# One PSUM tile for all of the attention, an FFN output that lands by token, four search steps in every body, and two FFN pieces at a body's front

## What is computed

```python
x = x + _xattn(_layernorm(x), ctx, ctx, mask, WQ, bQ, WK, bK, WV, bV, Wp, bp)
x = x + _ffn(_layernorm(x), W1, b1, W2, b2, gamma, beta, Wr, br)
# _xattn: softmax((Q K^T) * mask) / sqrt(d) @ V, then @ Wp + bp
# _ffn:   probs = softmax(layernorm(x) @ Wr + br)
#         out = sum_e probs[e] * (gelu(x @ W1s[e] + b1s[e]) @ W2s[e] + b2s[e])
# W1s[1:], b1s[1:], ...: the largest 5% by |w| times 0.2, the smallest 5% times 1.8
```

## Time and profile before

| | us |
|---|---|
| median of 3 runs | 839.43 |
| lowest and highest | 836.33, 840.46 |
| the profiled execution | 837.27 |
| its span, first to last instruction | 835.5 |
| PE busy / weight loads busy | 718.3 / 605.3 |
| DVE busy / ACT busy / POOL busy | 525.4 / 316.0 / 291.2 |

### The profile page before, as it was taken

One profiled execution on the slowest core, in us unless ns is written; L12 is line 12 of the kernel. 1 busy time (PEld: TensorE's weight loads), 2 busy tenths in 40 slices (PEclk: granted clock), 3 DMA queues, 4 the chain that ended last, 5 costly groups with the idle time before them and its releaser, 6 DMA issues.

```text
span 835.5 us, 15333 instructions
## 1 busy us (share of the span) xinstructions
PE 718.3 (86%) x5346; PEld 605.3 (72%) x5346; DVE 525.4 (63%) x1327; ACT 316.0 (38%) x428; POOL 291.2 (35%) x288
## 2 busy tenths in 40 slices
PE   3438758898898859989989989989896999999996
PEld 2426656787787748878878878888674888888884
DVE  3698468547857976776776776666499334333441
ACT  1302201333442324444444444443352444555442
POOL 2246034225625732762753753735381000000000
PEclk9758757679799959999999999979897999999999
DMA  5851510420341115044044033023020122222121
GB/s 162 192 136 51 112 43 22 96 66 27 101 109 32 51 54 115 27 111 105 26 119 98 25 104 90 26 76 102 26 77 15 61 76 75 75 75 72 41 63 50
DMA packets 128571, 62.36 MB, mean 75 GB/s; under 512 B 101520, under 2 KB 118800, under 8 KB 128528
## 3 DMA queue, kind: packets, MB, share of 16 engines
q1 hardware_dynamic: 128528, 61.81, 28.0%
HBM read 34.51 MB, written 23.09 MB: 69 GB/s over the span
## 4 chain that ended last, share of the span: by engine, by line
PE 66%; DVE 21%; issue 6%; POOL 4%; ACT 1%; DMA 0%; DVEq 0%; ACTq 0%; POOLq 0%
PE ps_y L337 8%; PE ps_y L338 8%; PE ps_y L339 8%; PE ps_l L337 7%; PE ps_l L338 7%; PE ps_l L339 7%; PE ps_m L591 6%; DVE ind L1212 5%; POOL xh L993 3%; PE ps_m L678 3%; PE ps_s L337 2%; PE ps_s L339 2%; PE ps_s L338 2%; DVE region_a L1113 2%; PE ps_m L626 2%
## 5 line engine op out<-in xcount | busy, mean ns | idle before, releaser
L874 ACT ACTIVATE region_b<-ps_l,bias 128x512 f32<-128x512 f32 x128 | 88.1, 689 | 196.7 <-PE ps_l L339 193.7
L1025 POOL TENSOR_TENSOR region_c_lo<-region_b,region_c_hi 128x512 fp32r<-128x512 f32 x64 | 98.0, 1547 | 142.9 <-ACT region_c_hi L877 142.9
L1212 DVE TENSOR_SCALAR ind<-key,cand 128x2048 bf16<-128x2048 uint16 x124 | 116.1, 978 | 5.0 <-PE ps_m L678 3.0
L1442 DVE TENSOR_TENSOR region_c_lo<-region_b,region_c_hi 128x512 fp32r<-128x512 f32 x64 | 44.1, 692 | 109.0 <-ACT region_c_hi L877 104.6
L337 PE MATMUL ps_l<-x2s_hi,w_hi 128*128 128x512 f32 x256 | 108.0, 422 | 5.0 <-DVE x2s_lo L1076 5.0
L678 PE MATMUL ps_m<-ones_bf,ind 128*128 128x1 bf16 x1984 | 63.2, 164 | 51.6 <-DVE ind L1212 48.2
L337 PE MATMUL ps_y<-region_c_hi,w_hi 128*128 128x512 f32 x256 | 103.9, 406 | 1.6 <-POOL region_c_lo L1025 1.6
L678 PEld LDWEIGHTS ps_m<-ones_bf,ind 128*128 128x128 bf16 x1984 | 58.4, 99 | 62.7 <-DVE ind L1212 56.4
L338 PE MATMUL ps_l<-x2s_lo,w_hi 128*128 128x512 f32 x256 | 103.5, 404 | 0.0
L339 PE MATMUL ps_l<-x2s_hi,w_lo 128*128 128x512 f32 x256 | 103.4, 404 | 0.0
L339 PE MATMUL ps_y<-region_c_hi,w_lo 128*128 128x512 f32 x256 | 101.6, 397 | 0.0
(11 more groups left out here) (173 smaller groups left out, 1232.8 us busy)
## 6 DMA issues: line engine op xcount, KB each, us to landing
acc_scr<-acc SPq DMA_DIRECT2D x8, 514.0 KB, 4.8
acc<-acc_scr SPq DMA_DIRECT2D x8, 514.0 KB, 3.3
xa<-in_x SPq DMA_DIRECT2D x8, 512.0 KB, 5.2
q_scr<-qn_hi SPq DMA_DIRECT2D x16, 256.0 KB, 4.5
q_scr<-qn_lo SPq DMA_DIRECT2D x16, 256.0 KB, 4.6
qs_hi<-q_scr SPq DMA_DIRECT2D x8, 512.0 KB, 4.1
qs_lo<-q_scr SPq DMA_DIRECT2D x8, 512.0 KB, 5.0
x<-in_x SPq DMA_DIRECT2D x32, 128.0 KB, 3.6
```

The costliest lines, as they stand in the source:

```text
L874: act.activation(g[:, f % 4, :], ps_l[:, f % 2, :], ACT.Gelu_apprx_tanh, bias=bias[:, e, f:f + 1]).then_inc(s["gelu"].handle, 1)
L1025: pool.tensor_tensor(gs[1][:, f % 4, :], g[:, f % 4, :], gs[0][:, f % 4, :].bitcast(F32), ALU.subtract).then_inc(s["g_lo"].handle, 1)
L1212: dve.tensor_scalar(ind[s % 2][:], key[:, key_of[rnd][s], :], cand[:, s:s + 1], None, ALU.is_le).then_inc(ind_ready.handle, 1)
L1442: dve.tensor_tensor(gs[1][:, f % 4, :], g[:, f % 4, :], gs[0][:, f % 4, :].bitcast(F32), ALU.subtract).then_inc(s["g_lo"].handle, 1)
```

## The change

1. **PSUM.** The turned probabilities, the turned queries' input and the queries move from `ps_l` and `ps_y` into `ps_s`, which also holds scores, turned output, projection and turned x2. `ps_l` and `ps_y` belong to the FFN alone. New waits keep the users of `ps_s` apart.
2. **FFN output by token.** `output` takes the GELU tile as the stationary operand and W2 as the moving one: 12 matmuls of 256 columns in place of 6 of 512. `bias_y` and `turn_y` go. b2 is added by a new `base` on VectorE (4 operations a batch).
3. **Scores.** `sc` gets four tiles and the exponential is taken in place. All four scores of batch i+1 are made at the end of body i, all four of batch 0 in the prologue.
4. **Search.** There are four steps in each of bodies 0 to 6 and none in body 7. Four `ind` tiles; the small arrays take one comparison and one reduction; `decide` forms the next candidate in its second operation.
5. **Order.** Two FFN pieces, h(0) and h(1), stand at the front of a body, and the GELUs stand between the attention's copies on ScalarE. `mix` stands before `mask_scores(i+1, 3)`.
6. **Prologue.** The keys of batch 0 go straight into `kbd` (`load_first_keys`, 16 small DMAs). The loads are reordered, and the steps stand between the masks.
7. `normalise_output` takes one four-dimensional operation a tile.
8. The weights' perturbation takes up `probabilities`, `base` and the b2 row between its parts.

```diff
-            for m in range(DC):
-                mm = three(pe, ps_y[:, m, :], [w[:, f * D + m * P:f * D + (m + 1) * P] for w in w2s],
-                           [t[:, f % 4, :] for t in gs], f == 0, f == FC - 1)
+            for t in range(NT):
+
+                mm = three(pe, ps_y[:, t // 2, (t % 2) * D:(t % 2) * D + D], [a[:, f % 4, t * P:(t + 1) * P] for a in gs],
+                           [w[:, f * D:(f + 1) * D] for w in w2s], f == 0 and t % 2 == 0, f == FC - 1 and t % 2 == 1)
...
         def turn_queries_input(b):
 
             wait(pe, ln[0]["xhat"], b)
-            wait(pe, ex[0]["mixed"], b - 3)
+            if not isinstance(b, int) or b > 0:
+                wait(pe, pT_ready, b - 1, 1)
...
             wait(pe, xT_lo, b)
+            if not isinstance(b, int) or b > 0:
+                wait(pe, pT_ready, b - 1, 2)
...
-        def turn_probs(b, j):
+        def turn_probs(b, j, last=False):
+
             wait(pe, p_exp, b, j + 1)
             if j == 0:
-                wait(pe, ex[0]["g_hi"], b - 2)
-            elif j < NT - 1:
+                wait(pe, s_masked, b)
+            elif j == 1 and not last:
+                wait(pe, xT_lo, b + 1)
+            elif j == 2 and not last:
+                wait(pe, q_lo, b + 1)
+            else:
                 wait(pe, pT_ready, b, j)
...
+            h(0)
+            h(1)
+            turn_probs(i, 0, last)
+            if not last:
+                turn_queries_input(i + 1)
+            values(i, 0)
+            c(0)
+            turn_probs(i, 1, last)
+            if not last:
+                queries(i + 1)
+            values(i, 1)
+            t(0)
+            h(2)
...
+            probs(i, NT - 1)
+            if not first:
+                router_exp(i - 1)
+            more_gelu(0)
             turned(i, 0)
...
+            if not last:
+                decide(k + 2)
+                mask_scores(i + 1, 0)
+                mask_scores(i + 1, 1)
+                compare(k + 3, rnd)
+            low_x2(i)
+            if not last:
+                mask_scores(i + 1, 2)
+            logits(i)
+            if not last:
+                counts(k + 3)
+            if not first:
+                mix(0, i - 1)
+            if not last:
+                mask_scores(i + 1, 3)
+                decide(k + 3)
```

More of the change, by code:

```diff
@@ L694, in keys_values @@
                 mm.then_inc(kv_product, 1)
-        def step(k):
-            count(k, 0)
-            count(k, 1)
-            total(k)
         pe.wait_ge(ld_ctx, 16)
@@ L708, in _ @@
         pe.wait_ge(ctx_lo, 1)
-        keys_values(0, ps_s)
+        keys_values(0, ps_l)
         turn_queries_input(0)
-        keys_values(1, ps_l)
         pe.wait_ge(proj_lo[0], 1)
         queries(0)
+        keys_values(1, ps_y)
         pe.wait_ge(kk_in, 16 * B)
+        pe.wait_ge(kv_biased, KC)
         for c in range(DC):
             for k in range(KC):
-                mm = pe.transpose(ps_s[:, c, k * P:(k + 1) * P], kk[:, k, c * P:(c + 1) * P], ident[:])
+                mm = pe.transpose(ps_l[:, c, k * P:(k + 1) * P], kk[:, k, c * P:(c + 1) * P], ident[:])
         mm.then_inc(k_turned, 1)
         pe.wait_ge(consts_ready, 5)
-        for k in range(AHEAD):
-            step(k)
+        count(0)
+        pe.wait_ge(proj_lo[3], 1)
+        pe.wait_ge(k0_lo_in, 16 * HH)
+        wait(pe, q_lo, 0)
+        scores(0, 0)
+        total(0)
+        scores(0, 1)
+        count(1)
+        scores(0, 2)
+        total(1)
+        scores(0, 3)
         pe.wait_ge(route_w, 2 * DC)
@@ L727, in _ @@
         mm.then_inc(route_sum, 1)
-        pe.wait_ge(proj_lo[3], 1)
-        pe.wait_ge(k_lo, 1)
-        scores(0, 0)
-        scores(0, 1)
-        scores(0, 2)
+        count(2)
+        total(2)
         pe.wait_ge(route_ready, 1)
         def body(i, rnd, first=False, last=False):
-            k = step_of(i, rnd)
-            more = not isinstance(i, int) or i + 2 < B
-            turn_probs(i, 0)
-            scores(i, 3)
-            values(i, 0)
-            if not last:
-                turn_queries_input(i + 1)
-            turn_probs(i, 1)
-            count(k, 0)
-            if not last:
-                queries(i + 1)
-            values(i, 1)
-            count(k, 1)
-            turn_probs(i, 2)
-            turn_probs(i, 3)
-            total(k)
-            values(i, 2)
+            k = step_of(i)
             def h(f):
@@ L1059, in body @@
                 normalise(0, i + 2, xa)
+            for f in range(3, FC - 2):
+                low(f)
+            rsqrt(1, i)
+            normalise(1, i, x2)
+            low(6)
+            if not last:
+                shift(i + 1, 0)
+            low(7)
+            if not last:
+                shift(i + 1, 1)
+            router_rsqrt(i)
             if not last:
@@ L1362, in body @@
                     dve.tensor_copy(key[:, 2 + n, :], halfword(wraw[:, n, :], 0)).then_inc(key_ready, 1)
-            compare(k + 1, 0, rnd)
+            else:
+                probabilities(i - 1)
+                base(0, i - 1)
             normalise_output(i, 2)
-            normalise_output(i, 3)
-            if not first:
-                probabilities(i - 1)
-            low_output(i)
-            compare(k + 1, 1, rnd)
-            counts(k + 1)
-            add_residual(i)
-            stats(1, i, x2)
-            decide(k + 1)
-            compare(k + 2, 0, rnd)
-            compare(k + 2, 1, rnd)
-            counts(k + 2)
-            decide(k + 2)
-            if rnd == 0 or last:
-                step(k + 3, rnd)
-            if more:
+            if not isinstance(i, int) or i + 2 < B:
                 wait(dve, x_in, i + 2)
@@ L1383, in body @@
             if not last:
+                counts(k + 1)
+            normalise_output(i, 3)
+            if not last:
+                decide(k + 1)
+                compare(k + 2, rnd)
+            low_output(i)
+            if not last:
+                counts(k + 2)
+            add_residual(i)
+            stats(1, i, x2)
+            if not last:
+                decide(k + 2)
                 mask_scores(i + 1, 0)
-            logits(i)
-            if not last:
                 mask_scores(i + 1, 1)
+                compare(k + 3, rnd)
             low_x2(i)
@@ L1423, in last_expert @@
             split_x2(0)
-            for part, s in ((slice(0, FC), 4), (slice(FC, FC + DC), 6)):
-                perturb(bias[:, 1, part], bias[:, 0, part], sabs[:, part], tier[:, part], s, pb_ready)
             wait(dve, ex[0]["y_step"], B - 1)
             split([t[:] for t in w2s], wagain[:, 1, :], pw_hi, 2, pw_lo)
-            probabilities(B - 1)
-            mix(0, B - 1, ps_s)
+            mix(0, B - 1)
         pipeline(dve, body, second_round, last_expert)
@@ L1436, in perturbed_expert @@
                 split_x2(b)
+                mix(1, b - 1)
             for f in range(FC):
-                if f == 2 and not first:
-                    mix(1, b - 1, ps_m)
                 wait(dve, s["g_hi"], b, f + 1)
```

479 lines of the change are left out of this document (240 added, 239 removed).

## The result

The changed kernel took **909.41 us** (median of 4 runs, 906.8 to 911.69). Beside them the kernel before took 837.88 (4 runs, 836.27 to 840.46). The ratio is 1.085, with a 95% interval from 1.080 to 1.090. The forecast was 904, slower, in a range from 864 to 934.

A forecast was written before the change was run, and what follows sets the result against it. Full bodies and expert 1 were taken as bound by TensorE, the prologue and body 0 by latency and queues. Terms 17.4 + 10.8 + 50.6 - 8.8 + 2.6 - 7.6 = +65 took the 835.5 span to 900.5, median 904; range 864 to 934.

The forecast's parts named there:

- the wait at the front: At a full body's start TensorE waits about 7 us for ScalarE's copy of the turned probabilities, behind a 9.4 us chain.
- Six full bodies: Bodies 1 to 6: 75 us each, from 59.0 work and 15.9 waits, plus 6 once; 456 in all, +50.6 us.
- the second round: Second round of the search, on VectorE behind the fourth mask: 13.1 us before, only 6 remain, in one full body.
- The wait at `total`: At a full body's end TensorE waits 4 us for VectorE's counts, and 1 more ahead of the last count.
- The smaller waits: Within a full body, TensorE's waits at turned probabilities, queries' low part, second step's total and queries' input: together 3.9 us.
- the price of the clock: In a full body, half-rate values, count and queries after the front's wait: up to +5 us, as a bound only.
- Four comparisons near the end: VectorE's four comparisons near a body's end, slowed beside GpSimd's low parts and shifts: 5 to 6 us, not 2.8.
- Prologue: Before the bodies: mask at 69 to 70, then 21 us on VectorE; first turned probabilities at 90, not 72.6: +17.4 us.
- Body 0: First body, without FFN to fill waits: first copy 8 us after the transposes, 75.5 us against 64.7, +10.8.
- Body 7 and the way to expert 1: Body 7: 52 us from 60.8, -8.8; weights' perturbation on VectorE before expert 1: 37 instead of 34.5, +2.6.
- Expert 1: Last stage: output by token costs nothing, dropping `turn_y` gives 0.7 in each of 7 batches, the end 2.6: -7.6 us.
- the work alone sets the body: Rival, chance 0.12: the front's chain is covered, full bodies take 62 us, and the kernel takes 807.

The follow-up runs named there:

- e5_order: e1_front with an FFN piece and the last output piece moved between narrow matmuls on TensorE, and the fourth mask ahead of `mix` on VectorE: 855.7 us.
- e4_prologue: e1_front with batch 0's mask loaded before the queries' store, search steps ahead of the scores, and GpSimd normalising batch 1 before the first subtraction: 844.7 us.
- e8_two: The changed kernel with the values normalised in two three-dimensional operations a tile again: 909.6 us, against 907.4 for the changed kernel beside it.
- e6_both: The edits of e4_prologue and e5_order together on e1_front: 830.7 us, ratio 0.989 to the kernel before.
- e10_input: e9_total with normalisation and the queries' input's low part ahead of a body's first comparisons on VectorE, and the first count behind the queries on TensorE: 816.4 us.
- e1_front: The changed kernel with ScalarE's copies of the first turned probabilities and queries' input ahead of the first GELUs, the former also ahead of the fourth exponential: 867.0 us.
- e9_total: e6_both with the last total behind the next body's first FFN piece on TensorE, and last counts and fourth mask ahead of the router's logits on VectorE: 837.7 us.

## Why the prediction was right

The sign, the size and the main mechanisms were right: 904 forecast and 909 measured, with the wait at the front and the late prologue where they were forecast. But in the largest term two errors of the same size cancelled, and that part is luck.

- **Six full bodies**: 456 forecast, 456.2 measured, of them 74.6 to 74.9 us for three of the five without the second round. *Split wrong.* I had put 59.0 us of work and 15.9 of waits. It was 65.2 of work and 9.7 of waits. The wait at the front was 6.1 (forecast 7), through the chain forecast: 9.35 us from mask to transposes, of 9.4. The wait at `total` was 0.3 to 0.4 in four of the six bodies and 1.7 and 1.9 in the other two, not 4, and the one ahead of the last count was nil, not 1. The smaller waits were 3.2 of 3.9. So the waits had been put 6.2 too high. Against that stands the price of the clock, the step that failed: I named up to +5 as a bound for it and put nothing in the sum, and TensorE was busy for 6.2 us more than forecast, with 17 us at 1.2 GHz at the front and 3 more at the end. By the 57.7 us of the same matmuls at 2.4 GHz (e5_order) the clock even cost 7.5, and the work had been put 1.3 too high. The missing wait at `total` and the slow clock are in part the same thing: in the body from 400.2 the scores ahead of it ran at half rate from 468.0 on and so came nearly as late as VectorE did, while in the body from 243.3, where no half-rate stretch stood there, the wait was 1.7. The second round added 7.5 us to its body, not 6.
- **Four comparisons near the end** took 4.91 us (forecast 5 to 6), but not by being slower each, as I had reckoned. The shortest, the median and the longest of the four, in ns:

```profile
L1220 DVE TENSOR_SCALAR ind<-key,cand x4: 741/742/2926, 460.2 to 464.4; 128x2048 bf16<-128x2048 uint16 x4
```

  One took 2.93, beside a low part and a subtraction of GpSimd, and three took 0.74, as they do alone. The pair of 2.71 in the earlier trace rows is made in the same way, of 2.04 and 0.74. What was mis-sized for the wait at `total` is when VectorE would be through the logits: 21.6 us after the projection's end, not 24, while TensorE was through the scores at 21.5, not 20.6.
- **Prologue**: first turned probabilities at 90.55 (90), first mask at 68.7 (69 to 70). Right, and e4_prologue shows that the cause was the order, as the step had it: with it changed, 71.4. Inside the chain on VectorE two terms were off and cancelled: the comparisons weren't slowed (2.74 us for four, twice, with no 2.5 on top), and the two decisions took 2.5 each, not 2 together, since in both one operation took 1.89 beside a subtraction of GpSimd.
- **Body 0**: +14.7 (+10.8). The wait at L562 was 9.2 (8), and the whole body ran at 0.58 of the clock, 0.68 in the earlier trace rows. Here too the clock was left out.
- **Body 7 and the way to expert 1** (626.1 to the first hidden matmul at 713.24): 87.1 against 95.3 before, -8.2, where -8.8 and +2.6 make -6.2. Body 7, to the end of its last output matmul, was shorter by 11 (forecast 8.8), and the path from there to expert 1 longer by 3 (forecast 2.6).
- **Expert 1**: 713.24 to 906.8 is 193.6, against 197.5: -3.9 (-7.6). *A term mis-sized.* The batches follow each other after 23.17 us, where they did before after 23.28, as the `mix` of two neighbouring batches shows, after and before:

```profile
761.51 1.66 DVE L1201 SCALAR_TENSOR_TENSOR acc<-ps_y,acc 128x256 f32<-128x256 f32 x4 [0.41 <-PE ps_y L344]
...
784.68 1.66 DVE L1201 SCALAR_TENSOR_TENSOR acc<-ps_y,acc 128x256 f32<-128x256 f32 x4 [0.41 <-PE ps_y L344]
```

```profile
738.36 1.66 DVE L1192 SCALAR_TENSOR_TENSOR acc<-ps_m,acc 128x256 f32<-128x256 f32 x4
...
761.64 1.65 DVE L1192 SCALAR_TENSOR_TENSOR acc<-ps_m,acc 128x256 f32<-128x256 f32 x4
```

  The gain is 0.11 a batch, not 0.7. `turn_y` gave its 1.0 back, but I had taken the new form as equal from two rounded figures. 96 narrow matmuls of 0.12 us are 11.5, 48 wide ones of 0.229 are 11.0, and a piece has changes of width more. The other 3 of the 3.9 came at the two ends of the stage.
- **The four-dimensional operation**: hidden, as forecast, or at most 2 us (e8_two).
- **What the Trainium skill said of GpSimd and VectorE.** The router's addition, which I left out, took 1.9 us beside a subtraction in each of bodies 1 to 6, where it took 0.19 alone in body 7. The four operations of `base` took 4.67 once beside the low parts, where they take 1.67 alone. This is the contention that the Trainium skill ("GPSIMD Engine Reference", "Key points") states for instructions with two SBUF inputs. The trace agrees with it. Leaving it out did matter: in two of the six full bodies of the changed kernel the waits of 1.7 and 1.9 us at the total stood behind that addition, and in e6_both the wait of 1.6 did.
- **The table load.** 478.80 to 480.09, 1.29 us: as in the earlier trace rows nothing of the 1.38 us of draining shows that the Trainium skill ("ScalarE: Activation LUTs", "What ACT_TABLE_LOAD costs") adds.

Of the rivals, *the work alone sets the body* was the interesting one: with nothing but orders changed and no operation taken out (e10_input) five bodies are at 62 to 64 us, near the 62 that it named, and the kernel at 816. It is what the changed kernel could have been. As written, three things kept it from that: ScalarE's order at the front (42 us), the order of the prologue (22), and the places of the narrow matmuls and of VectorE's work around a body's start (28 more, from e4_prologue to e10_input).

## What to carry to other kernels

When several stages come to share one PSUM tile, put the copy that frees the tile first on its engine, ahead of everything that only feeds later work: here that order alone was 42 of the 71.5 us lost, and no operation had to change. Give the clock a term of its own in the sum wherever a wait stands next to narrow matmuls, and not only a bound: here it cost 6 to 7.5 us a body. But don't tie it to the length of the wait, for e1_front took 4.2 us of waits out of a body and got 2.6 back from the clock, and in e5_order it cost 7.5 or nothing beside the same waits. And judge an edit that only removes a wait by who arrives late next, for e9_total took away 2 us of waits a body, up to 3.7 came up elsewhere, and it was 7 us slower.

## What the runs showed of the hardware

- The same loop body with the same waits took 63.4 us at a granted clock of 1.00 and 70.9 at 0.86 in one execution (e5_order). In the full bodies of the changed kernel the stretches at 1.2 GHz lasted 3 to 27 us. They began in a wait of TensorE, or with no wait behind the router's and the count's matmuls, which are 8 columns and 1 column wide (at 468.0).
- One of VectorE's comparisons (one tensor input) took 0.74 us alone. In the changed kernel 106 of the 124 took 0.74 to 0.92. The other 18 took 1.8 to 2.9, and each of them ended 0.55 to 0.58 us after a subtraction or a low part of GpSimd (two inputs of 512 or 1024 columns) had ended.
- Operations with two SBUF inputs were held in the same way: the router's addition of 128x32 took 0.19 us alone and 1.90 beside a subtraction, ending 0.05 us after it, and in e9_total the small comparison took 1.25 instead of 0.18.
- Small loads cost SyncE 0.64 us each in its queue: sixteen of them held back all that stood behind them by 10 us.
